# A two-layer gated cross-attention kernel: one ring of key/value slots, an f32 context spill, normalisation on GpSimd, and other places for the weight work

## What is computed

```python
x = x + tanh(g_xattn[0]) * xattn_A(ctx, layernorm(x), mask)   # 8 heads of 64, keys = 112 latents + 375 context rows
x = x + tanh(g_ffn[0])   * moe_A(layernorm(x))                # 8 experts, top 2, hidden 512, silu(h1) * h3
x = x + tanh(g_xattn[1]) * xattn_B(ctx, layernorm(x), mask)   # 16 heads of 64
x = x + tanh(g_ffn[1])   * ffn_B(layernorm(x))                # activations to 8 bits, weights ternary, 1024 wide, conv of 3
```

## Time and profile before

| what | value |
|---|---|
| timed runs | 1536.02, 1542.29, 1548.83 us; median 1542.29 |
| profiled execution, span | 1538.1 us (the page gives its span as its time) |
| busy share | PE 83%, PEld 65%, DVE 69%, ACT 64%, POOL 72% |
| DMA | 239.96 MB, mean 156 GB/s; 388848 of 438329 packets are under 512 B |

### The profile page before, as it was taken

How to read it: one execution, slowest core, us unless ns; L and a number is a source line. 1 busy time by engine, 2 the same in 40 slices (tenths; PEclk the granted TensorE clock), 3 DMA queues, 4 the chain that set the end, 5 groups by cost and what they waited for, 6 DMA issues and landing times.

```text
span 1538.1 us, 45142 instructions
## 1 busy us (share of the span) xinstructions
PE 1278.3 (83%) x16918; PEld 994.2 (65%) x16918; DVE 1053.8 (69%) x2830; ACT 979.1 (64%) x2319; POOL 1107.9 (72%) x1359
## 2 busy tenths in 40 slices
PE   0778787679878989878999999899999999998852
PEld 0556565557667866656887887667676676766642
DVE  4768788977556656665666666777777777877634
ACT  2778787456455666554656566678777777777631
POOL 4768788687557755466777776788878888787653
PEclk9989999879999989989999999999999999999965
DMA  9599997486999954368999997344555444555310
GB/s 314 134 193 235 246 239 174 83 221 188 218 233 252 233 95 97 73 159 171 247 258 231 269 247 181 79 97 98 105 91 94 90 105 94 106 82 91 79 32 6
DMA packets 438329, 239.96 MB, mean 156 GB/s; under 512 B 388848, under 2 KB 420320, under 8 KB 429024
## 3 DMA queue, kind: packets, MB, share of 16 engines
q1 hardware_dynamic: 408216, 178.51, 55.7%
q10 hardware_dynamic: 26824, 51.22, 10.6%
q0 software_dynamic: 3072, 7.34, 1.6%
HBM read 107.78 MB, written 35.50 MB: 93 GB/s over the span
## 4 chain that ended last, share of the span: by engine, by line
PE 39%; ACT 13%; DVE 12%; POOL 11%; issue 9%; DMA 9%; DVEq 3%; SPq 2%; ACTq 1%; POOLq 0%
PE bank_ring L1088 9%; PE bank_ring L1126 6%; PE bank_ring L1074 5%; PE bank_out L1107 5%; DVE scores L1340 4%; DMA expert_up<-experts_up 4%; ACT scores L849 4%; PE bank_x L1187 3%; POOL probs L654 3%; PE bank_scores L1048 3%; ACT probs L856 3%; PE bank_x L1140 3%; DMA probs_turned<-probs 3%; ACT values L876 2%; DMA context<-in_ctx 2%
## 5 line engine op out<-in xcount | busy, mean ns | idle before, releaser
L654 POOL TENSOR_TENSOR probs<-scores,probs 112x487 f16<-112x487 f32 x384 | 425.0, 1123 | 234.2 <-ACT probs L856 229.1
L849 ACT ACTIVATE scores<-scores,score_min 112x487 f32<-112x487 f32 x384 | 265.8, 693 | 121.0 <-DVE score_min L1340 118.2
L1357 DVE SCALAR_TENSOR_TENSOR values<-bank_ring,values 128x512 f16<-128x512 f32 x192 | 132.4, 689 | 216.4 <-ACT values L876 216.3
L1340 DVE CUSTOM_DVE_ANT_0 scores<-bank_scores,mask 112x487 f32<-112x487 f32 x384 | 238.1, 657 | 2.9 <-PE bank_scores L1048 2.9
L856 ACT ACTIVATE probs<-scores 112x487 f16<-112x487 f32 x384 | 214.2, 604 | 24.4 <-DMA probs_turned<-probs 9.0
L1088 PE MATMUL bank_ring<-weights,kv_B 128*128 128x128 f16 x3072 | 198.3, 223 | 1.2 <-DVE keys L1352 1.2
L876 ACT ACTIVATE values<-bank_ring 128x512 f16<-128x512 f32 x192 | 112.9, 588 | 128.9 <-PE bank_out L1107 125.2
L1088 PEld LDWEIGHTS bank_ring<-weights,kv_B 128*128 128x128 f16 x3072 | 187.2, 100 | 10.5 <-DVE keys L1352 2.0
L1107 PE MATMUL bank_out<-values,probs_turned 128*128 128x64 f16 x4608 | 171.9, 195 | 17.7 <-issue 11.4
L1074 PE MATMUL bank_ring<-kv_B,weights 128*128 128x488 f16 x768 | 181.0, 372 | 0.0
L1107 PEld LDWEIGHTS bank_out<-values,probs_turned 128*128 128x128 f16 x4608 | 160.1, 100 | 21.4 <-issue 14.0
(11 more groups left out here) (230 smaller groups left out, 2470.9 us busy)
## 6 DMA issues: line engine op xcount, KB each, us to landing
expert_up<-experts_up SPq DMA_DIRECT2D x43, 1024.0 KB, 5.5
expert_down<-experts_down SPq DMA_DIRECT2D x43, 512.0 KB, 6.6
raw_weights<-in_weights ACTq DMA_DIRECT2D x8, 1536.0 KB, 10.7
experts_up<-expert_up ACTq DMA_DIRECT2D x8, 1024.0 KB, 4.4
raw_weights<-in_weights ACTq DMA_DIRECT2D x6, 1024.0 KB, 8.0
probs_turned<-probs SPq DMA_TRANSPOSE x384
context_turned_B<-kv_B ACTq DMA_DIRECT2D x16, 375.0 KB, 8.7
kv_B<-context_turned_B ACTq DMA_DIRECT2D x16, 375.0 KB, 3.7
```

Source lines behind the costliest of these rows:

```text
L654: pool.tensor_tensor(PR[:, u % 4, 1, 0:KEYS], S[:, u % 4, 0:KEYS], PR[:, u % 4, 0, 0:KEYS], ALU.subtract).then_inc(probs_split, 1)
L849: act_e.activation(S[:, u % 4, 0:KEYS], S[:, u % 4, 0:KEYS], ACT.Exp, bias=rmin[:, u % 4:u % 4 + 1], scale=-1.0, accum_out=rsum[:, g % 2, ...
L1340: dve.tensor_tensor_reduce(out=S[:, u % 4, 0:KEYS], in0=bS[u % 2][0:TOK, 0:KEYS], in1=mask[:, m, 0:KEYS], scale=1.0, scalar=3.0e38, op0=AL ...
L1357: dve.scalar_tensor_tensor(vN[:, j % 2, 1].rearrange("p t d -> p (t d)"), bank("v", j)[:], 1 / WSCALE, vN[:, j % 2, 0].rearrange("p t d -> ...
```

## The change

Read as parts, in the order of the prediction:

1. **Start.** The zeroing of the expert rows leaves the start: it becomes 6 DMAs of 3 tiles in steps 4 to 9 and 5 DMAs of 5 tiles in steps 57 to 61, issued on SP's queue behind the step's transposes, from one row of zeros. x is loaded in smaller parts (sequences 6 to 15 in step 0). The remainders of sequence 0's context wait for the split of attention A's weights, because the f32 affine of POOL now lies in the tile that holds these weights.
2. **Stage P.** One tile `kv` with four slots serves both layers. `p_apply` moves from DVE to POOL. The latents' affine is made once, by DVE straight from PSUM (four tensor_scalars for A, two for B), and ACT only rounds it (two activations for A, one for B); POOL only takes the remainder. The mask is an instruction of its own, with its own semaphore, for which DVE waits; `kv_ready` is raised by the latents' remainder. From sequence 4 on all of stage P lies two steps earlier (one for sequences 2 and 3).
3. **Spill.** Layer B's rounding leaves layer A. ACT sends `rawT` itself (f32, one piece of 3000 B a partition) to DRAM; in layer B it is fetched into `rawT` (step `start_b(n)`-9) and rounded there (ACT in step `start_b(n)`-7, POOL's two `split_context` in step `start_b(n)`-6).
4. **Other weights.** The experts keep two chunks a step; their raw weights lie in the space of attention B's weights. Those come in two loads of 1.5 MB (steps 37 and 39, pieces of 2 KB) and one of 1 MB (step 58) and are split one a step in steps 53 to 68. The FFN's weights are loaded in steps 58 and 60, summed in steps 62 to 65 and made ternary in steps 68 to 75.
5. **Scatters** of batch 0 go four a step, and its first tile is in step 37. The first fetch of expert weights goes behind the step's transposes.

The diff, cut to its core:

```diff
-SCATTERS = (3, 4)
+SCATTERS = (4, 4)
+KV_SLOTS = 4
+ZERO_TILES = (3, 5)
+ZERO_STEPS = (4, 57)
...
+P_FIRST = {"norm": -9, "rest": -9, "rstd": -8, "apply": -8, "turn0": -8, "turn1": -7, "lat": -6,
+           "hi": -5, "lo": -5, "lat_hi": -4, "lat_lo": -5}
+P_AT = {"load": -14, "norm": -12, "rest": -11, "rstd": -10, "apply": -9, "turn0": -8, "turn1": -7, "lat": -6,
+        "spill": -6, "hi": -5, "lo": -4, "lat_hi": -4, "lat_lo": -3}
...
+    lead = (0, 0, 1, 1)[n] if n < 4 else 2
+    return max(4 * n + P_AT[name] - lead, FIRST_STEP + 1)
...
-WSUM_STEP = 31
-FFN_SUM_STEP, FFN_STEP = 26, 32
-L1_STEP = 41
+L1_STEP = 53
+FFN_SUM_STEP, WSUM_STEP, FFN_STEP = 62, 67, 68
+L1_ORDER = (0, 2, 4, 6, 8, 10, 1, 3, 5, 7, 9, 11, 12, 13, 14, 15)
...
-        kv_dram = dram("context_turned_B", (NSEQ, 128, KB, 2, CTX), F16)
+        kv_dram = dram("context_kept", (NSEQ, 128, KB, CTX), F32)
...
-        kv = {0: sb("kv_A", [128, 2, KB, 2, 512], F16), 1: sb("kv_B", [128, 2, KB, 2, 512], F16)}
+        kv = sb("kv", [128, KV_SLOTS, KB, 2, 512], F16)
+        no_row = sb("no_row", [128, 2 * DIM], F16)
...
+            def zero_rows(b, i):
+                rows = xs[b].rearrange("(p t) c -> p t c", p=128)
+                at = ZERO_PIECES[b][i]
+                n = min(ZERO_TILES[b], TILES[b] - at)
+                sp.dma_start(rows[:, at:at + n, :],
+                             no_row[:].rearrange("p (o c) -> p o c", o=1).to_broadcast([128, n, 2 * DIM]))\
+                    .then_inc(rows_zeroed[b], 16)
...
+            def p_apply(n):
+                r = rs["P"]
+                pool.wait_ge(rstd_ready["P"], n + 1)
+                for t in range(CT):
+                    last = pool.tensor_scalar(ctxb[0:CP, n % 2, t, :], ctxb[0:CP, n % 2, t, :],
+                                              mv["P"][0:CP, t, 0:1], r[0:CP, t:t + 1], ALU.subtract, ALU.mult)
+                last.then_inc(ctx_normed, 1)
...
             def split_context(n, kb, layer):
...
                 if n == 0 and kb == 0:
                     pool.wait_ge(vectors_loaded, 48)
+                    pool.wait_ge(l0_split, L0_CHUNKS)
...
             def split_latents(layer, n):
-                pool.wait_ge(x1_drained, X1_AT[("bp"[layer == 0] + "_lat", n)])
+                pool.wait_ge(lat_hi[layer], n + 1)
+                at = slot(layer, n)
                 if layer == 0:
...
+                    pool.tensor_tensor(latq[:, n % 2, :, 1], lata[:, 0], latq[:, n % 2, :, 0], ALU.subtract)
+                pool.tensor_tensor(kv[:, at, :, 1, 0:TOK], lata[:, 1], kv[:, at, :, 0, 0:TOK], ALU.subtract)\
+                    .then_inc(kv_ready[layer], 1)
...
             def spill_context(n):
-                act_e.wait_ge(ctx_lo[1], 2 * n + 2)
-                act_e.dma_start(kv_dram[n], kv[1][:, n % 2, :, :, TOK:KEYS]).then_inc(spilled[n % 2], 16)
+                act_e.wait_ge(x1_drained, X1_AT[("p_turn", n, 1)])
+                act_e.dma_start(kv_dram[n], rawT[:]).then_inc(spilled, 16)
...
+                act_e.dma_start(rawT[:], kv_dram[n]).then_inc(turned_loaded, 16)
...
                     if j + 2 in (4 * n, start_b(n)):
+                        pe.wait_ge(ctx_lo[layer], 2 * n + 2)
                         pe.wait_ge(kv_ready[layer], n + 1)
-                        if layer:
-                            pe.wait_ge(kvb_loaded[n % 2], 16 * (n // 2 + 1))
...
+                if u // 2 in (4 * seq_of(u // 2), start_b(seq_of(u // 2))) and u % 2 == 0:
+                    dve.wait_ge(mask_ready, layer_of(u // 2) * NSEQ + seq_of(u // 2) + 1)
...
                     if n:
+                        dve.wait_ge(ctx_hi[0], 2 * (n - 1) + kb + 1)
                         dve.wait_ge(ctx_lo[0], 2 * (n - 1) + kb + 1)
-                        dve.wait_ge(ctx_lo[1], 2 * (n - 1) + kb + 1)
+                        dve.wait_ge(spilled, 16 * n)
                     dve.tensor_copy(rawT[:, kb], bX1[:, 0:CTX]).then_inc(x1_drained, 1)
...
-                    dve.tensor_copy(latT[:], bX1[:, 0:KB * TOK].rearrange("p (k t) -> p k t", k=KB))\
-                        .then_inc(x1_drained, 1)
+                    for i, c in ((0, V_GLAT), (1, V_GATED)) if layer == 0 else ((1, 8 + V_GLAT),):
+                        for kb in range(KB):
+                            scale, shift = latent_vec(c, kb)
+                            last = dve.tensor_scalar(lata[:, i, kb], bX1[:, TOK * kb:TOK * kb + TOK], scale, shift,
+                                                     ALU.mult, ALU.add)
+                    last.then_inc(x1_drained, 1)
```

More of the change, by code:

```diff
@@ L56 @@
 TILES = tuple((2 * TOK * (b - a) + EXPERTS * 127) // 128 for a, b in BATCHES)
-SCATTERS = (3, 4)
+SCATTERS = (4, 4)
 XR_SLOTS = 10
-ZERO_DMAS = sum(-(-t // XR_SLOTS) for t in TILES)
+KV_SLOTS = 4
+ZERO_PIECES = tuple(tuple(range(0, t, n)) for t, n in zip(TILES, (3, 5)))
+ZERO_TILES = (3, 5)
+ZERO_STEPS = (4, 57)
 def is_pair(j):
@@ L762, in _ @@
                     split_hidden(m[1], m[2], m[3])
-                if (j + 4) % 4 == 0 and 0 < (j + 4) // 4 < NSEQ:
-                    split_context((j + 4) // 4, 1, 0)
+                for n in range(NSEQ):
+                    if n and j == p_step(n, "lo"):
+                        split_context(n, 1, 0)
+                    if j == start_b(n) - 6:
+                        split_context(n, 1, 1)
                 if is_pair(j):
@@ L937, in round_latents @@
             def round_latents(n):
                 act_e.wait_ge(x1_drained, X1_AT[("p_lat", n)])
[L939 to L945 removed]
+                if n >= 2:
+                    act_e.wait_ge(x0_filled, X0_AT[("q", 4 * (n - 2) + 3)])
@@ L966, in _ @@
                 for n in range(2, NSEQ):
-                    if j == max(4 * n - 14, FIRST_STEP + 1):
+                    if j == p_step(n, "load"):
                         load_context(n)
-                if (j + 2) % 4 == 0 and 0 <= (j + 2) // 4 < NSEQ:
-                    spill_context((j + 2) // 4)
                 for n in range(NSEQ):
-                    if j == start_b(n) - (6 if n < 2 else 7):
+                    if j == start_b(n) - 9:
                         reload_context(n)
@@ L995, in _ @@
                 load_weights(j)
+                for n in range(NSEQ):
+                    if j == p_step(n, "spill"):
+                        spill_context(n)
                 for t in late(j - 1):
@@ L1001, in _ @@
                     copy_result(m[1][1], m[1][2])
-                if (j + 5) % 4 == 0 and 0 <= (j + 5) // 4 < NSEQ:
-                    round_context((j + 5) // 4)
-                if (j + 4) % 4 == 0 and 0 <= (j + 4) // 4 < NSEQ:
-                    round_latents((j + 4) // 4)
+                for n in range(NSEQ):
+                    if j == p_step(n, "hi"):
+                        round_context(0, n)
+                    if j == start_b(n) - 7:
+                        round_context(1, n)
+                    if j == p_step(n, "lat_hi"):
+                        round_latents(n)
                 for n in range(NSEQ):
@@ L1669, in _ @@
                     split_v(j - 1)
-                for n in range(NSEQ):
-                    if j == p_step(n, -8, -9):
-                        p_apply(n)
                 if j == -8:
```

360 lines of the change are left out of this document (184 added, 176 removed).

## The result

The changed kernel took 1562.12 us (median of four runs, 1551.12 to 1570.29) against 1544.63 for the kernel before: ratio 1.0108, 95% interval [1.0056, 1.016]. The forecast was 1506, with 1550 as its upper end; the sign is wrong. The profiled execution, the fastest of the changed kernel's four, has a span of 1549.1 us against 1538.1, so 11.0 us are to be explained, and 47 against the sum of -36.

The account below looks back on a forecast made before the run. No engine bounds the whole span: layer B without tiles is close to PE, layer A loses time to stage P, weight work and transfers. Terms sum to -36 on 1538.1, giving 1502.1, plus 4.2 carried over: 1506 us, range 1455 to 1550.

Parts of the forecast that it names:

- the wait for the mask, -18: Layer A, ten sequences' starts: PE's 29.5 us of waits for POOL's mask go; six of ten taken whole, -18 us.
- less work in layer A, -9: Steps 0 to 31: per sequence POOL loses 3.4 us, ACT 1.4, DVE 1.4; -9 us, between 0 and -27.
- Start, -9: Before the first query: it goes at about 33 us instead of 43.9, -11; 2 given back for DVE's copy behind the spill.
- The first fetch: Tile steps: one scatter more a step and the first tile a step earlier put at 0; the fetch's move not named.
- The rule weighed: GpSimd and DVE operations with two SBUF operands exclude each other; POOL's -3.4 us could be about zero, the sum changing little.
- Spill and tile steps, -16: Layer A's tile steps: 512 of 887 small DMA pieces go; -16 us, between -29 and +11.
- Other weights, 0: FFN's work leaves steps 26 to 39 for 62 to 75, attention B's chunks go to 53 to 69: -14 and +14.
- Zero rows, +6: Zeroing transfers: +4 us in steps 4 to 9 before the transposes, +2 for the rest; between 0 and +18.
- Layer B, +10: Sixteen sequences in layer B: ACT's added rounding and lag behind POOL's blocks, 0.3 us each; +10 us, between 0 and +57.
- DMA as the bound of layer A: Rival, no change: freed waits in layer A become waits for transposes; 0, 1542 us; chance 0.18.
- POOL becomes the bound in layer B: Rival, slower: POOL's two blocks in step `start_b(n)`-6 delay ACT and DVE, 80 us; 1576 us; chance 0.13.

Follow-up runs that it names:

- the mask alone: Kernel before with only the mask made behind the latents' split, with a semaphore of its own; 1552.12 us, ratio 1.003 to the kernel before.
- three edits: Changed kernel with experts' weights over 30 steps, x loaded in step 5 (expert 1's in step 1), first fetch at step head; 1528.0 us, 0.9899.

## Why the prediction was wrong

**The two terms that failed: "the wait for the mask, -18" and "less work in layer A, -9".** Seven of the ten waits for the mask, 20.6 of their 29.5 us, lie in steps 1 to 31, so 12.6 of the 18 do; with -9 and with +4 for the zero rows that is -18 for these steps. Measured were +2.4, a gap of 20 us of the 47. The waits did go, and ACT's and DVE's work fell, but I summed waits and asked "what is late next" only of the engines: "each engine is at about 0.8". POOL's own relief, which was to be the largest, did not come: its work in these steps grew by 2.0 us. The DMA share of 0.86 stood in the same row and was left to a rival. Runs show that the transfers are next: steps 4 to 23 are 14.6 us shorter without the loads of six experts, with the same work on the engines, and the mask alone gains nothing. The sign of being wrong was named: waits of PE or ACT for transposes in place of the mask's. The kernel before has the pace of two chunks too, and took 148.0 us for the same steps. So the experts' transfers explain why nothing was gained; why the steps became longer is not settled. The zero pieces are 4.4 and 5.8 us of it in two runs. But step 13 alone took 11.7 to 13.1 us in all six kernels with two chunks and all loads, and 6.2 before, so a stall eats there what the other steps gain: with the zero rows at the start the other 19 of the 20 are 6.1 us shorter than before.

**"Start, -9".** Two failures in one term. The first query was forecast at 33 us and came at 36.9, 7 us earlier than before and not 11; with the normalisation back on DVE it came at 34.5, so this is 2.3 of the missing 4. Then "I give 2 back" for the new wait of DVE on the spill: step 0 grew by 11.4. I took its landing from the median of the old spill, 8.7 us, and did not look at what is issued beside the new one within 5 us: two expert loads and x, 4.1 MB. It landed after some 15 us. Together the term is +5.3 in place of -9, 14 us of the gap. The sign to look for, a new wait at the copies to `rawT`, was named.

**The first fetch, priced 0.** "One scatter more a step and the first tile a step earlier move work without adding any" did not price the move of the fetch behind the transposes at all. It costs 9.6 us in step 79 and 3.4 in steps 36 and 37. Step 37 took 21.5 us, against the sign "no tile step of 20 us".

**The rule weighed.** I let the exclusion of POOL by DVE go because "the sum changes by little". I had also taken the normalisation as 0.53 us an instruction from the affine's row; POOL took a mean of 1.31, against DVE's 0.35 at the start. POOL's -3.4 a sequence was thus about zero: the figure that I had put beside the rule, but not for its reason, since an instruction with no weight split beside it took 1.22 us already. The Trainium skill (SBUF — State Buffer, Who interferes with whom) says that a DVE instruction with two inputs in SBUF and a GpSimd instruction that reads SBUF shut each other out, and so spoke against this part of the change. The trace is compatible with it and does not prove it: three such instructions took 3.65 us with no split beside them, 4.74 where one overlapped their start, and 1.04 on DVE. So at most 1.1 of these 3.7 us are the exclusion, and 2.6 are the instruction's own length on POOL. (DVE's -1.4 a sequence adds up to -1.6 from the figures given for it, which changes nothing.)

**What held.** "Spill and tile steps, -16": steps 40 to 55 are 16.8 us shorter, and no step there takes 20 us. "Other weights, 0": steps 56 to 78 grew by 7.2 against +14 and +2, and steps 32 to 39 fell by 3.3 against -14 (without the late fetch 6.7); the ternary operations cost less than 2 us a step. "Zero rows, +6": the +4 of it in steps 4 to 9 was 5.8 in steps 4 to 23, with 4.7 saved at the start. "Layer B, +10": 6.1 from step 80 on, and the new waits of DVE and ACT for POOL there were under 1 us each, 15.8 us in all.

**The rivals.** DMA as the bound of layer A came closest: 0 by its working, and by its mechanism. What it lacked are the late fetch (13 us) and the wait for the spill in step 0 (11.4). That POOL becomes the bound in layer B, which I had as the way to a slower kernel, did not happen. The chances were wrong in the same way: slower had 0.12, nearly all of it for POOL, and none for the three places that made it so.

## What to carry to other kernels

Before a removed wait is booked as gain, look for the resource that is fullest in that stretch, the DMA queues among them, and book only what that one lets through. A transfer that something newly waits for, or that is moved in its queue, is priced beside all that is issued within its landing time on the other queues, not by a median over the whole span. A change can hold a gain of 1% and show a loss of 1%: three edits of place and pace brought 1.0108 to 0.9899.

## What the runs showed of the hardware that was not expected

A wait for one transpose of the probabilities can grow to 15 us. In the run with the fetch at the head this made step 9 last 30.2 us; an expert's store and load had been issued in step 8. The waits of its window of 114 to 146 us:

```profile
PE bank_out L1170 <- DMA probs_turned<-probs: 25.5, 2, 14.6
ACT probs L929 <- DMA probs_turned<-probs: 24.6, 2, 14.9
```

The same window in 40 slices of 0.8 us, the share of the DMA engines in tenths and the rate:

```profile
DMA  3699999989969925928899136799899890000299
GB/s 116 78 153 42 34 57 45 70 36 24 49 35 73 96 12 171 444 75 315 312 401 300 47 106 265 257 447 424 217 309 282 271 66 32 33 17 26 35 260 315
```

From the fourth slice on the engines of the DMA are mostly nine tenths busy for some 8 us and move 24 to 73 GB/s; later slices at the same share move 282 to 447, and one again 66. In the run with thin zero rows step 7 took 25 us in the same manner (windows of all engines):

```profile
92.80:117.90 25.10, 5.38 (x62) 4.01 (x61) 5.78 (x17) 6.37 (x16) 4.20 (x5) 0.66 1.12 125
117.90:124.60 6.70, 6.53 (x88) 4.96 (x87) 5.21 (x13) 4.76 (x11) 6.40 (x10) 1.00 0.81 171
```

PE works 5.38 of these 25 us, and its mean granted clock there is 0.66 against 1.00 in step 8. The length is chance in this place: the run with the later loads of attention B has the same program up to step 36 as the one with three edits, and its step 7 took 19.1 us against 12.3. Such a stall stood in one or two of the steps 7 to 13 of most runs (the expectations say step 10 for all; in two runs it is step 9), one or two steps behind an expert's store and load. It did not go with x moved or with the zero rows moved, and the run without the loads had no step over 8.8 us in steps 4 to 23.

The stall of step 13 is not chance: it stood in all six kernels with two chunks a step and all loads (11.7 to 13.1 us) and in no other (6.2 to 8.1). What sets these six apart can be read from ACT's queue. In the changed kernel step 11 issues an expert's store and load and the next context's load together, and step 12 the spill:

```profile
137.63 0.34 ACTq L873 DMA_DIRECT2D experts_up<-expert_up  x1
...
138.50 0.95 ACTq L860 DMA_DIRECT2D weights<-in_weights  x1
139.63 1.04 ACTq L840 DMA_DIRECT2D context<-in_ctx  x1
143.56 1.94 ACTq L845 DMA_DIRECT2D context_kept<-context_turned  x1
```

In the kernel before the context and the spill are issued in steps 9 and 13, at 118.40 and 146.25 us, away from the expert's in step 11, at 132.01; it is this change that puts them beside it. With 1.6 chunks a step it is the expert's transfers that move, from step 11 to step 13. So the pace and the meeting of the transfers were changed together, and no run separates them: a kernel with two chunks a step and the contexts a step later was not tried. Against the meeting as the whole cause: in the kernel before the two meet in steps 5 and 17, and the two steps behind took 9.3 us at most. With the mask's edit that kernel had one step of 12.1 us too, step 15, behind a context in step 13 and an expert in step 14. Why the rate falls stays open as well; a run without the stores was not tried.

An instruction of GpSimd that subtracts and multiplies by a value of each partition took 1.22 us for 256 elements (L659 at 19.74 us), and one that multiplies and adds took 0.72 for 375 (the mean of the 64 of L671 in the changed kernel).
